# Attention heads that stay transposed: transfers and ScalarE and GpSimd in place of TensorE transposes, and a new merge of four lanes

## The reference

```python
# layer 0: rotary self-attention, 16 heads of 16
o = softmax(q @ k.T * 16**-0.5) @ v ; out = o @ w_proj + b_proj
# layer 0: gated mixing of x with the context (8 heads of 32), cumulative decays, norm per head
# layer 0: quantized FFN: bitlinear(relu(g)**2 * u, w_down), rows to 8 bits, weights to -1, 0, 1
# layer 1: self-attention (16 heads), cross-attention on the context (16 heads), FFN 256-1024-256 with relu
```

## Time and profile before

| | us |
|---|---|
| three runs | 1613.53, 1617.63, 1618.95 |
| their median | 1617.63 |
| the profiled execution | 1622.2 |
| its span, first to last instruction | 1620.4 |
| PE busy | 1465.2 (90%) |
| DVE busy | 1183.2 (73%) |
| ACT busy | 950.7 (59%) |
| POOL busy | 225.4 (14%) |
| mean granted TensorE clock | 0.969 of 2.4 GHz |

### The profile page before, as it was taken

How to read it: one execution, slowest core, us unless ns; L and a number is a source line. 1 busy time by engine, 2 the same in 40 slices (tenths; PEclk the granted TensorE clock), 3 DMA queues, 4 the chain that set the end, 5 groups by cost and what they waited for, 6 DMA issues and landing times. The chain is left out here.

```text
span 1620.4 us, 31692 instructions
## 1 busy us (share of the span) xinstructions
PE 1465.2 (90%) x12482; PEld 972.9 (60%) x12482; DVE 1183.2 (73%) x2103; ACT 950.7 (59%) x1701; POOL 225.4 (14%) x233
## 2 busy tenths in 40 slices
PE   7588799899999879899999888998999988898998
PEld 4155556557766556557767555565776656465577
DVE  5978887865568888974765888866565788888632
ACT  3378466674466757566355666656545586655752
POOL 6011100002221011002212210000122111100100
PEclk9699989999999999999999898999999999999999
DMA  8430113322121021521321011331322101133200
GB/s 273 139 102 2 52 47 105 118 60 79 53 69 51 2 63 48 152 67 58 119 73 53 1 47 33 93 108 50 111 72 66 53 2 46 47 97 110 70 1 26
DMA packets 115074, 114.34 MB, mean 71 GB/s; under 512 B 9842, under 2 KB 100722, under 8 KB 114930
## 3 DMA queue, kind: packets, MB, share of 16 engines
q1 hardware_dynamic: 114610, 111.28, 22.4%
q10 hardware_dynamic: 320, 1.05, 0.3%
HBM read 68.91 MB, written 42.99 MB: 69 GB/s over the span
## 5 line engine op out<-in xcount | busy, mean ns | idle before, releaser
L1170 DVE TENSOR_REDUCE nm<-psum 128x4 f16<-128x1024 f32 x384 | 455.1, 1223 | 100.3 <-PE psum L767 99.2
L1005 ACT ACTIVATE PB<-psum 128x1024 f32<-128x1024 f32 x288 | 288.3, 1024 | 87.1 <-PE psum L786 85.7
L804 PE MATMUL psum<-PB,V 128*32 128x256 f32 x2304 | 206.8, 390 | 7.4 <-ACT PB L1005 5.2
L1347 POOL TENSOR_TENSOR XO<-XO,row_b 128x512 f32<-128x512 f32 x80 | 103.2, 1300 | 749.8 <-ACT YX L976 749.8
L767 PE MATMUL psum<-QK 48*128 48x256 f16 x1536 | 140.4, 280 | 46.8 <-DVE nm L1170 22.7
L786 PE MATMUL psum<-QK 49*128 49x256 f16 x1536 | 138.3, 277 | 21.4 <-ACT PB L1005 5.3
L767 PEld LDWEIGHTS psum<-QK 48*128 48x128 f16 x1536 | 58.9, 96 | 109.8 <-DVE nm L1170 38.8
L786 PEld LDWEIGHTS psum<-QK 49*128 49x128 f16 x1536 | 54.2, 95 | 111.4 <-issue 42.1
L930 PE MATMUL psum<-YX,W 128*128 128x256 f32 x512 | 120.0, 385 | 0.0
L804 PEld LDWEIGHTS psum<-PB,V 128*32 128x32 f32 x2304 | 79.9, 110 | 62.6 <-issue 20.0
L938 PE MATMUL psum<-W,PB 128*128 128x256 f32 x512 | 116.3, 382 | 0.0
(11 more groups left out here) (171 smaller groups left out, 2675.4 us busy)
## 6 DMA issues: line engine op xcount, KB each, us to landing
QK<-heads_dram SPq DMA_DIRECT2D x96, 512.0 KB, 3.8
heads_dram<-U SPq DMA_DIRECT2D x288, 128.0 KB, 2.0
XO<-in_x SPq DMA_DIRECT2D x16, 256.0 KB, 3.2
YX<-in_ctx SPq DMA_DIRECT2D x16, 256.0 KB, 3.4
out<-XO SPq DMA_DIRECT2D x16, 256.0 KB, 2.5
W<-in_w SPq DMA_DIRECT2D x2, 1024.0 KB, 6.9
heads_dram<-PB ACTq DMA_DIRECT2D x4, 256.0 KB, 9.4
W_gu<-in_w_down SPq DMA_DIRECT2D x1, 1024.0 KB, 5.6
```

Of the source, the lines that this page charges most:

```text
L804: ins = pe.matmul(b[SLOT * j:SLOT * j + SLOT, at:at + TOK], value(L, t, PAIRS * e + u, HEADS, HD, SLOT), src, start=(t == 0), stop=(t == T ...
L1005: act.activation(weights_of(L, unit), b[:, 0:1024], ACT.Exp, scale=HD ** -0.5)\
L1170: dve.tensor_reduce(nm[L][:, :, :, unit].rearrange("p t e -> p e t"), b[:, 0:1024].rearrange("p (e t k) -> p e t k", e=2, t=TT), AX.X, ALU ...
L1347: pool.tensor_tensor(stream(L, it), stream(L, it), row_b[:, occ:occ + 1, :].to_broadcast([P, TT, DIM]), ALU.add).then_inc(xb_ready[L], 1)
```

## The change

- V is laid out with 32 columns a head, value columns and ones in turn (`VA`, `ones`). A product of `pv` then gives 32 rows, 16 of values and 16 that all hold the sum, in turn. Its number and shape stay.
- New step `spread` (SP): four transfers of 64 rows by 2x256 float32 copy the even rows of U to OT and the odd rows to `sums` (the other half of YX). Both tiles then hold 128 rows in the order that proj wants.
- Step `heads` is now ACT (natural logarithm of `sums`, then exp of its negative, both 128x512) and POOL (OT times `sums`, 128x512). Step `oT`, the eight and the four transposes, both DVE instructions and the ACT copy are gone. proj waits for POOL.
- The cross-attention's k waits for `spread`; the next x is loaded once `quant` of the batch before is done; the square in `mixnorm` takes over the wait for the store.
- At the start SP issues lane 0's x, W_qkv, the other x, and then the four contexts. The seven further loads are issued by ACT, behind its four and behind the arrival of W_qkv, and ahead of its first copy.
- `FILL` gives each use of a PSUM bank a number of products of the identity with 128x256 float32 of constants, written to that bank ahead of the real ones. They stand behind the wait for the bank and ahead of the wait for the operands. The digits sum to 180. Nothing reads what they write.
- `TURNS` and `PLACES` are new for all engines. Small buffers share one tile.

```diff
-    "exp": "pe act", "pv": "pe act", "heads": "pe dve", "oT": "pe act", "proj": "pe dve act", "norm": "dve",
+    "exp": "pe act", "pv": "pe act", "spread": "sp", "heads": "act pool", "proj": "pe dve act", "norm": "dve",
...
         add("pv", a, 3)
+        add("spread", a)
         add("heads", a)
         if a == 1:
             add("qk", 2, 1)
             add("stack", 2, 1)
             add("v", 2)
-        add("oT", a)
...
+FILL = (
+    "2301000000000120300100022030032101001000200000000010000000000000000010000001003001000000000100100000"
...
-        V = lanes("V", [P, TT * HEADS * (HD + 1) + SLOT])
+        V = lanes("V", [P, TT * HEADS * 2 * HD])
...
-
-        VA = [v[:, 0:TT * HEADS * (HD + 1)].rearrange("p (t h c) -> p t h c", t=TT, c=HD + 1) for v in V]
+        sums = [v[:, 0].rearrange("p (k t) -> p k t", k=KT) for v in YX]
+
+        VA, ones = ([v[:, :].rearrange("p (n d c) -> p n d c", d=HD, c=2)[:, :, :, n] for v in V] for n in range(2))
...
+        def value(lane, t, e, u):
+            at = (t * HEADS + PAIRS * e + u) * 2 * HD
+            return V[lane][:, at:at + 2 * HD]
...
+                fill_at[key] = int(fills[len(use_at)])
...
                 load_x(0, 0)
-                load_c(0, 0)
                 load(qkv_loaded, (W_qkv[0][:, :, :], kt_major(w_qkv0)))
                 for L in range(1, LANES):
                     load_x(L, 0)
+                for L in range(LANES):
                     load_c(L, 0)
-
-                sp.wait_ge(c_loaded[2], 16)
-                load(raw_loaded, (raw[2].rearrange("p (k n) -> p k n", k=IT), kt_major(w_down)),
-                     (raw[0].rearrange("p (k n) -> p k n", k=KT), kt_major(w_gate)), (W_1[:, :, :], kt_major(w_up)))
-                load(rows_loaded, (row_b[:, :, :], rows.rearrange("(a n) d -> a n d", a=1).to_broadcast([P, 7, DIM])))
-                load(staged_in, (staged[0].rearrange("p (k n) -> p k n", k=KT), kt_major(w_qkv1)[:, :, 0:2 * DIM]),
-                     *[(staged[n].rearrange("p (k n) -> p k n", k=KT), kt_major(w)) for n, w in ((1, wq), (2, wk))])
...
                 elif name == "loadx" and it:
-                    sp.wait_ge(turned[L], nth(TURNED, it - 1, "oT2"))
+                    sp.wait_ge(turned[L], nth(TURNED, it - 1, "quant"))
...
+                elif name == "spread":
+                    sp.wait_ge(u_ready[L], it * U_USES + U_AT[occ] + 2)
+                    for home, other in ((OT, 0), (sums, 1)):
+                        for g in range(2):
+                            sp.dma_start(home[L][64 * g:64 * g + 64, :, :], U[L][other:P:2, g:4:2, :])\
+                              .then_inc(spread[L], 16)
...
-                return place(it, name, L, occ, unit, j)
+                b = place(it, name, L, occ, unit, j)
+                for _ in range(fill_at[it, name, L, occ, unit, j]):
+                    pe.matmul(b[:, 0:2 * P], ident, cst[:, 0:2 * P], start=True, stop=True)
+                return b
...
-                elif name == "heads" or name == "mixnorm":
-                    b = claim(*step)
-                    groups = 4 if name == "heads" else 2
-                    pe.wait_ge(u_ready[L], it * U_USES + (U_AT[occ] + 2 if name == "heads" else U_MIX + 1))
+                elif name == "mixnorm":
+                    b = claim(*step)
+                    pe.wait_ge(u_ready[L], it * U_USES + U_MIX + 1)
                     for t in range(TT):
-                        for g in range(groups):
-                            at = (t * groups + g) * P
...
-                elif name == "oT":
-                    b = claim(*step)
-                    pe.wait_ge(o_ready[L], it * ATTN + occ + 1)
-                    filled(turn_x(outputs(L, it), b), *step)
...
-                    pe.wait_ge(turned[L], nth(TURNED, it, f"oT{occ}"))
+                    pe.wait_ge(o_ready[L], it * ATTN + occ + 1)
...
-            act.wait_ge(set_pool, 4 + 2 * LANES)
+            act.wait_ge(set_pool, 4 + LANES)
...
-                if name == "permute":
+                if name == "raws":
+                    act.wait_ge(qkv_loaded, 16)
+                    load(raw_loaded, (raw[2].rearrange("p (k n) -> p k n", k=IT), kt_major(w_down)),
+                         (raw[0].rearrange("p (k n) -> p k n", k=KT), kt_major(w_gate)), (W_1[:, :, :], kt_major(w_up)))
+                elif name == "tables":
+                    load(rows_loaded, (row_b[:, :, :], rows.rearrange("(a n) d -> a n d", a=1).to_broadcast([P, 7, DIM])))
+                    load(staged_in, (staged[0].rearrange("p (k n) -> p k n", k=KT), kt_major(w_qkv1)[:, :, 0:2 * DIM]),
+                         *[(staged[n].rearrange("p (k n) -> p k n", k=KT), kt_major(w)) for n, w in ((1, wq), (2, wk))])
...
-                            act.wait_ge(o_ready[L], it * ATTN + 2)
+                            act.wait_ge(spread[L], (it * ATTN + 2) * 64)
...
-                elif name == "oT":
-                    b = wait_full(act, *step)
-                    act.activation(flat2(OT[L][:, :, :]), b[:, 0:512], ACT.Copy).then_inc(turned[L], 1)
+                elif name == "heads":
+                    act.wait_ge(spread[L], (it * ATTN + occ + 1) * 64)
+                    log = own(act.activation(flat2(sums[L][:, :, :]), flat2(sums[L][:, :, :]), ACT.Ln))
+                    wait_own(log)
+                    act.activation(flat2(sums[L][:, :, :]), flat2(sums[L][:, :, :]), ACT.Exp, scale=-1.0)\
+                       .then_inc(inverse_ready[L], 1)
...
+                    if it == 0:
+                        act.wait_ge(scaled_w, SCALED.index("mean") + 1)
+                    else:
+                        act.wait_ge(stored[L], it * 16)
...
-                elif name == "heads":
-                    b = wait_full(dve, *step)[:, 0:1024].rearrange("p (h c) -> p h c", c=SLOT)
...
-                    inverse = own(dve.reciprocal(sums, b[:, :, HD]))
-                    wait_own(inverse)
-                    dve.tensor_tensor(outputs(L, it).rearrange("p t (h d) -> p (t h) d", d=HD), b[:, :, 0:HD],
-                                      sums.rearrange("p (h d) -> p h d", d=1).to_broadcast([P, TT * HEADS, HD]),
-                                      ALU.mult).then_inc(o_ready[L], 1)
...
+                setup(pool.memset(ones[L], 1.0))
...
+                elif name == "heads":
+                    pool.wait_ge(inverse_ready[L], it * ATTN + occ + 1)
+                    pool.tensor_tensor(flat2(OT[L][:, :, :]), flat2(OT[L][:, :, :]), flat2(sums[L][:, :, :]), ALU.mult)\
+                        .then_inc(o_ready[L], 1)
...
```

209 lines of the change are left out of this document (105 added, 104 removed).

## The result

| | before | after |
|---|---|---|
| median of the runs, us | 1618.01 | 1595.38 |
| lowest and highest | 1613.53, 1618.95 | 1593.44, 1597.43 |
| profiled execution, its span | 1622.2, 1620.4 | 1596.0, 1594.0 |

The changed kernel takes 0.9837 of the time before, interval 0.9800 to 0.9873: faster by 23 us (medians) to 26 us (ratio), where 59 were forecast. The time, 1595.38, lies within the stated 1508 to 1606 and 37 us above the forecast 1558.

What follows compares the result with a forecast made beforehand. PE bounds in seven of sixteen windows; in nine PE and DVE take turns. Terms -56 -14 +5 +3 +15 -8 -4 = -59 us from 1622.2 give 1563, median about 1558; range 1508 to 1606.

Steps and rivals of the forecast that it cites:

- Transposes and the pair: In each of 48 attentions, twelve transposes on PE and DVE's reciprocal and product go: -56 us, between -50 and -63.
- DVE's wait: DVE's 40.9 us of waiting for the transposes ahead of its reciprocals: a third goes, -14 us, ends 0 and -41.
- PE windows: Seven of sixteen 100 us windows, PE busy 94 to 99 us: PE bounds; expected to move earlier by about 5%.
- second rival: PE's saving handed to DVE: PE only waits longer, DVE's waits move ahead of the maxima; -5, about 1613 us; chance 0.05.
- The new chain: Between U and proj: 5.9 us instead of 2.96, covered by other lanes' PE work; +5 us, ends 0 and +139.
- slower rival: Transfers hold up the in-order queues of SP and ACT, 1.9 us exposed per attention: +27, about 1645 us; chance 0.12.
- More work on idle engines: ACT, POOL and SP's queue gain work without bounding; POOL's instructions can hold up DVE: +3 us, ends 0 and +10.
- The identity products: 180 cost 78 us of PE, a fifth on the path, +15 (0 to +78); clock regained, -8 (0 to -50).
- The start: Lane 0: first ACT copy at about 13, first maxima sooner, before 42 us; -4 us, ends +5 and -12.
- The merge: The new instruction order by itself: nothing, since both kinds of windows stay; ends ±40, a quarter of PE's idle time.
- The signs I had named: Instruction counts, engine totals, W_o's wait under 10 us, maxima before 42 us, PE windows earlier; reasons wrong if PE's idle grows.

Runs made afterwards that it cites:

- late loads: The changed kernel with the seven loads of ACT's queue moved behind its first three copies instead of ahead of them: 1597.91 us, ratio 0.9852.
- half products: The changed kernel with its 180 identity products 128x128 instead of 128x256, at the same places: 1599.64 us, ratio 0.9856.
- missing inverse: The changed kernel without ACT's logarithm and exponential of the sums, POOL multiplying by the sums, output not normalised: 1599.87 us, ratio 0.9856.

## Why the prediction was right or wrong

The sign was right, and so was that the new chain is hidden from PE; the forecast was 37 us too good. Three steps between measured kernels lead from before to after:

| step | forecast | measured |
|---|---|---|
| the work out of the old order | -70 | -20 |
| then the new chain, order and start, without products | +4 | +33 (1.0080 - 0.9876) |
| then the products | +7 | -39 (0.9837 - 1.0080) |
| together | -59 | -26 |

So two misses of 50 and 29 us too good and one of 46 us the other way partly cancelled: that the time lies in the range is in good part luck. Another path between the two kernels would split the 26 otherwise.

**Transposes and the pair (-56), DVE's wait (-14).** This is the step that failed first. Measured: -20 for ten of the twelve transposes and the pair, waits included. I had given PE windows PE's price and the others the smaller price of the two, as if each engine's saving counted where it is busy most. But most of PE's saving became idle time and a lower clock: 26 and 15 of 53 us. The second rival named just this ("PE's saving is handed to DVE"). I gave it 0.05, because few products stand in the PE windows, which says nothing of the saving. Its loss in clock it did not have either.

**The new chain (+5).** Its mechanism held: 1.0 us of waits ahead of W_o, and nothing gained by leaving out its two ACT instructions. The sizes of the transfers were off: issue 0.608 us for 0.47, landing 3.4 for 2.0. With 1.26 on ACT and 1.27 on POOL the chain is thus 7.8 us long, not 5.9, still under the median cover of 8.8 that I had counted. No run sets the new chain beside the old one in the new order, so its cost is not measured alone. In the old order the new chain makes the kernel 192 us slower. The slower rival had its place right, and in the new order its condition is not met: ACT's logarithm waits 22.1 us for landings in all.

**More work on idle engines (+3).** L1138 has a mean of 462 ns where L1111 had 457: 192 x 0.005 = 1 us, inside the end of 0 to 10.

**The identity products (+15 and -8).** Together +7 forecast, -39 measured: the second failed term, and its failure is the clock. The cost was about right: 92 us of PE for the 78 forecast, of which 14 lengthened the run by the bookkeeping above. What they gave back was 52 us of faster instructions, where I had 8 and bounded the whole clock at 50. That bound came from the clock of before, 0.969; the clock to compare with was that of the new kernel without products, 0.948. And I had held that most of the lost clock costs nothing, because PE waits there anyway. As the products cost 36 to 38 us in the old order, the gain is one of this order with these products in it, not of the clock alone.

**The start (-4).** The first copy came at 19.95, not 13, the first maxima at 48.76, not before 42, so the reasons given for the term were wrong. With the loads late the time is the same, so the delay costs nothing. What the new start is worth no run shows.

**The merge (0, ends ±40).** With chain and start +33 without products, where +4 was forecast; inside the ends, but the third term that missed. With the products -6. As neither chain nor start shows a wait of that size, most of it is likely the order's; that is argued, not shown. What the order alone does was not run: the new order around the old chain would need another plan of banks.

**The signs I had named.** The instructions of L817 are 64 instead of 448 (now L834), DVE is at 1147 (1133 forecast), ACT 985 (980), POOL 289 (287), the products are 360, W_o's wait is under 10 us. Whether the PE windows moved earlier can't be read from windows of 100 us at a gain of 1.6%. PE's idle time fell, from 155 to 116, which I had set as the test of my reasons; it passed and the reasons still were wrong, because products count as busy. Own work against idle time, as in the table of the result, shows what became of the saving.

What stays open: why an order takes in removed work so badly. That the lanes' chains run through PE, DVE and ACT alternately, so that an addition is always on some chain and a removal shortens only one of several of about equal length, would fit, but was only argued. So is the rival that the place counts and not the sign: work was put in at proj and taken out at `heads` and `oT`.

No version beat the changed kernel: late loads, half products and the missing inverse are within its interval.

## What to carry to other kernels

The price of an instruction put in is not the value of the same instruction taken out: in this finely interleaved order 63 us more, put in at proj, cost 61, and 53 us less, taken out where the change took them, gave 10. So price a removal by taking the work out of the kernel before in its own order, not by putting it back into the changed one. When work leaves PE, compare idle time and clock together, and count fillers apart from own work: here the clock went from 0.969 to 0.961 with the transposes out. Where fillers overlap other instructions, count only what is theirs alone. Then try fillers in the very order that will carry them, since the same 180 earned 39 us in one order and cost 36 in the other.

## What the runs showed of the hardware

- The issue of a weight load on ACT's queue took 3.68 and 4.38 us for the first two at 7.56 and 11.27 us, and 0.43 and 0.60 us for the same two issued at 21.84 and 22.31.
- A transfer from SBUF to SBUF of 128 KB (`YX<-U`) took 0.593 us at least to issue and 2.8 to 4.7 us to land, longer than the one to memory (2.0 median).
- Logarithm and exponential of 128x512 from and to SBUF took 0.630 us each on ACT, the copy from PSUM 0.598.
- Identity products of half the width (316 ns mean of an instruction against 426) gave the same time, at clocks of 0.980 to 0.987 in six executions against 0.985 and 0.986 in four.
